# A four-layer transformer on one core: in the first wide attention, the second norm's z and its turn each move one tick later

## The chip, the cores and the metric

The kernel runs on one core of a Trainium2 chip. The metric is the device time of one execution in microseconds (us); the figure of a kernel is the median of its runs. One further execution is recorded by the hardware profiler.

## What is computed

Sixteen sequences of 256 tokens with 128 channels pass through four blocks, each an attention and a feed-forward part on normalised input, added to the stream. The change lies in the first attention alone:

```python
x = x + _L0_attn_ref(_layernorm(x, axis=-1), gamma, w_q, w_kv, null_kv, q_scale, k_scale, w_out)

def _L0_attn_ref(x, gamma, w_q, w_kv, null_kv, q_scale, k_scale, w_out):
    ...
    xn = (x - mu) * jax.lax.rsqrt(var + LN_EPS) * gamma      # the second norm, after _layernorm
    q = (xn @ w_q) ...                                       # 16 heads of 64
    k, v = split(xn @ w_kv)
    ...                                                      # two null keys and values, l2norm of q and k,
    sim = q k^T * 8 + ALiBi, causal                          # softmax
    out = softmax(sim) v
    return out @ w_out
```

So the input is normalised twice, one norm after the other.

## The kernel before, in words

`Core` holds eight stages that run one behind the other; the first is `Wide(self, 0, 0, ...)`, the wide attention of kind 0. It treats the sequences b = 0 to 15 in a software pipeline whose step is called a tick. A sequence has an item "prep" that starts at tick 16b and four items "unit" (four heads each, u = 0 to 3) that start at ticks 16b + 8 + 4u. At each tick every live item issues its part k (ticks since its start). Within a tick the items are sorted by a rank, one for TensorE and ScalarE (`rank`), one for VectorE (`dve_rank`), one for GpSimd (`pool_rank`). The orders are fixed when the program is built; each engine works through its own list in order, and semaphores tie them together.

The prep of sequence b, in the kernel before:

- VectorE k = 0: mean and variance of x (`dve_stats`, L2770 and L2772), two token tiles of 128.
- GpSimd k = 1: 1/sqrt(variance) (`pool_rstd`, L2777 and L2779: an add and a power, per tile).
- VectorE k = 2: the first z (`dve_z`, L2785), then mean and variance of that z.
- GpSimd k = 3: 1/sqrt for the second norm. In tick 3 (mod 4) GpSimd first does a unit's part k = 3 (scale q and k to unit length, L1014 to L1021, and the null scores, L1007 and L1008), then this, then the sum of a unit's output into the stream (L982, four adds).
- VectorE k = 4: the second z (`dve_z`, z <- z), at rank 6, last in its tick.
- TensorE k = 6 (`zT_at`): two 128x128 transposes of z into PSUM (L2764, "ident,z"). ScalarE copies them, times gamma, as the high part of zT (L659); VectorE forms the low part (L797). On VectorE this is rank 1.
- The first user is part "qk" of unit 0 at tick 16b + 8. It waits for the low part (L2756 to L2758, products with wA).

What the engines do in the ticks around it (tick counted mod 16 within the sequence):

- Tick 4, TensorE: pv and row sums, v, qk. VectorE: null maximum, then the second z.
- Tick 5, TensorE: masks, st and mx scores (the last four of each group are "KH,QH"), qk, transposes of S. VectorE: two maxima (L892), squares' sum (L808), L849 and L850.
- Tick 6, TensorE: st and mx scores, **transposes of z**, the out product (L2761, "wO,OT", 16 matmuls), the turn of q (L2764, "ident,raw"). VectorE: two maxima (L892), three small steps on them (L902, L905, L910), **low part of zT**, L808, two products T (L861), low part of q (QL, L816).
- Tick 7, TensorE: turn of nm (L2764, "ident,nm", two transposes), turn of k (four). VectorE: low part of k (KL, L816).
- Tick 8, TensorE: pv ("P,V"), row sums ("P,one"), v, then qk of unit 0 of the new sequence.

PSUM's eight banks are given out in turn (`Psum.take`, ring G), in TensorE's order. A take waits until the reader of the take eight before it is done, since that one had the same bank. In tick 6 of the kernel before, the takes are st, st, mx, mx, zT, Y, Y, turn of q. The eighth take before zT is the first mx of tick 5, which VectorE reads by L892.

For sequence 0 the three VectorE parts of prep stand ahead of the pipeline (`pre_dve`, `is_early`), and `mid_dve` (small constants) stands in tick 7.

Of the kernel before, what the change touches and what calls it, by code (L numbers as in the profile page):

```python
# [29 lines left out]
def fv(a):  # L30
    return a.bitcast(F32)
# [96 lines left out]
class Wide:  # L128
# [9 lines left out]
    def __init__(self, K, s, kind, loads=(), behind=None):  # L138
        self.K, self.s, self.kind = K, s, kind
        self.causal = kind == 0  # L140
        if kind == 0:
            first, last, unit = 8, 13, 24
            self.tk = {"qk": 0, "turn": 6, "mx": 9, "v": 12, "mT": 15, "st": 17, "pv": 20, "sT": 21, "out": 22}
        else:
            first, last, unit = 6, 5, 19
            self.tk = {"turn": 0, "v": 2, "mx": 4, "mT": 7, "st": 8, "pv": 11, "sm": 15, "sT": 16, "out": 17}
        self.apart = (self.tk["st"] - self.tk["mx"]) // 4
        self.zT_at, self.sn_at = (6, 12) if kind == 0 else (4, 99)
        items = []
        for b in range(NSEQ):  # L150
            items.append((16 * b, 0, "prep", (b,), last))
# [118 lines left out]
    def is_early(self, name, a, k):  # L270

        if self.kind == 0:
            return name == "prep" and a[0] == 0 and k in (0, 2, 4)
        return self.kind == 2 and name == "prep" and a[0] < 2 and k in (0, 2, 4)

    def early_pe(self, pe, b, k):
# [486 lines left out]
    def dve_prep(self, dv, b, k):  # L763
        K, s, e = self.K, self.s, dv.e
        n = K.nb[s] + (4 * b if self.kind == 0 else 2 * b)
        za = self.z[(2 * b if self.kind == 0 else b) % len(self.z)]
        zb = self.z[(2 * b + 1) % len(self.z)]
        if self.kind == 2 and b == 0 and k == 3:
            dv.wait_ge(*K.ps.filled("bias"))
            e.tensor_copy(self.bias[:, :], K.ps.ap("bias")[:, 0:128]).then_inc(K.ps.out_of("bias"), 1)  # L770
        if self.kind == 0 and b == 0 and k == 7:
            K.mid_dve(dv)
        if self.kind == 0 and b == 0 and k == 12:
            K.late_dve(dv)
        if k == 0:
            K.x_ready(dv, s, b)
            for i in range(2):
                K.dve_stats(dv, n + i, K.XR[:, 2 * b + i, :])
        if k == 2:
            if self.kind == 2 and b >= 2:  # L780
                dv.wait_ge(*K.ps.filled("zT", s, b - 2))
            for i in range(2):
                K.dve_z(dv, n + i, za[:, i, :], K.XR[:, 2 * b + i, :])
            if self.kind == 0:
                dv.wait_ge(K.zs, n + 2)
                for i in range(2):
                    K.dve_stats(dv, n + 2 + i, za[:, i, :])
        if self.kind == 0 and k == 4:
            if b >= 2:
                dv.wait_ge(*K.ps.filled("zT", s, b - 2))  # L790
            for i in range(2):
                K.dve_z(dv, n + 2 + i, zb[:, i, :], za[:, i, :])
        if k == self.zT_at:
            dv.wait_ge(self.z_hi, b + 1)
            hi, lo, ps = self.zT[b % 3][:, 0:256], self.zT[b % 3][:, 256:512], K.ps.ap("zT", s, b)[:, 0:256]
            if self.kind == 0:
                i = e.scalar_tensor_tensor(lo, ps, K.pc("gamma"), fv(hi), ALU.mult, ALU.subtract)  # L797
            else:
                i = e.tensor_tensor(lo, ps, fv(hi), ALU.subtract)
            i.then_inc(K.ps.out_of("zT", s, b), 1)  # L800

    def dve_unit(self, dv, b, u, k):
        K, s, g, e, kind = self.K, self.s, 4 * b + u, dv.e, self.kind
# [121 lines left out]
    def pool(self, po):  # L925
        K, s, e = self.K, self.s, po.e
        K.stage_free(po, s)
        e.memset(self.one[:, :], 1.0).then_inc(self.one_in, 1)
        if self.kind == 0:
            e.memset(self.nvw[:, :], 0.0).then_inc(self.nv_zero, 1)  # L930
        for name, a, k in self.pool_order:
            if name == "prep":
                n = K.nb[s] + (4 if self.kind == 0 else 2) * a[0]
                if self.kind == 0 and k in (1, 3) and not self.is_early(name, a, k - 1):
                    for i in range(2):
                        K.pool_rstd(po, n + k - 1 + i)
                if self.kind == 2 and k == 0:
                    for i in range(2):
                        K.pool_rstd(po, n + i)
                if k == 3 and self.kind == 2:  # L940
                    self.pool_bias(po, a[0])
            elif name == "behind":
                a[0].pool(po, a[1], k)
            elif name == "ahead":
                K.stages[a[0]].early_pool(po, a[1], k)
            elif name == "null" and k == 2:
                b = a[0]
                xs = K.XR[:, 2 * b:2 * b + 2, :].rearrange("p t c -> p (t c)")
                po.wait_ge(self.summed, 4 * b + 4)
                po.wait_ge(*K.ps.read("nul", s, b))  # L950
                e.tensor_tensor(xs, xs, self.ny[b % 2][:, :], ALU.add).then_inc(self.nulled, 1)
            elif name == "unit":
                if self.kind == 0:
                    self.pool_unit(po, 4 * a[0] + a[1], k)
                elif self.part("st", k - 1) is not None:
                    self.pool_halves(po, 4 * a[0] + a[1], k - 1 - self.tk["st"])
                if k == self.tk["out"] + 1:
                    self.pool_sum(po, *a)
            elif name == "load":
                a[0].pool(po, k)  # L960
# [1632 lines left out]
class Core:  # L2593
# [252 lines left out]
    def pre_dve(self, dv):  # L2846
        e, nk, first = dv.e, self.nk, self.stages[0]
        dv.wait_ge(self.c_in["nk"], 16)
        e.tensor_tensor(nk[:, 16:32], nk[:, 0:16], nk[:, 0:16], ALU.mult).then_inc(self.nk_sq, 1)
        first.dve_prep(dv, 0, 0)  # L2850
        dv.wait_ge(*self.ps.filled("nk2"))
        e.tensor_scalar(nk[:, 160:176], self.ps.ap("nk2")[:, 0:16], 1e-24, None, ALU.max, ALU.bypass).then_inc(
            self.ps.out_of("nk2"), 1)
        self.a0_low(dv, 0).then_inc(self.a0_lo_v, 1)
        first.dve_prep(dv, 0, 2)
        self.a0_low(dv, 1).then_inc(self.a0_lo_v, 1)
        self.a0_low(dv, 2).then_inc(self.a0_lo_v, 1)
        first.dve_prep(dv, 0, 4)
        self.a0_low(dv, 3).then_inc(self.a0_lo_v, 1)
        dv.wait_ge(self.par_in, 16)  # L2860
        e.tensor_scalar(self.qs8[:, :], self.pc("qs"), 8.0, None, ALU.mult, ALU.bypass).then_inc(self.qs8_in, 1)
# [233 lines left out]
```

## Time and profile before

| | before |
|---|---|
| median of 3 runs | 2493.4 us (2490.78 to 2494.09) |
| profiled execution, its own time | 2489.93 us |
| its span, first to last instruction | 2488.3 us |
| TensorE busy, whole span | 93% |
| VectorE / ScalarE / GpSimd busy | 65% / 60% / 64% |
| mean granted TensorE clock | 0.981 of full speed |
| first stage (wide attention) | from the start to about 744 us |
| one sequence in that stage | 46.6 us |

Busy shares are averages over eight different stages. What matters for the change is which engine sets the pace of the first stage and what it waits for there.

### The profile page before, as it was taken

What the parts mean: (1) busy time and instruction counts of PE and PEld (TensorE: products, weight loads), DVE (VectorE), ACT (ScalarE), POOL (GpSimd) and SP (SyncE); (2) the same over time, 40 slices, a digit from 0 to 9 for tenths busy, and PEclk for the clock granted to TensorE, in tenths of its full rate; (3) what the DMA queues carried; (4) which work ended last, traced back from release to release, by engine and by line L of the source; (5) the groups of instructions that cost most, each with busy time, mean ns of one, the idle gap of its engine ahead of it and who ended that gap; (6) DMA issues with size and microseconds to landing.
All of it is one profiled execution on the core that took longest, in us unless ns stands there. A gap on an engine that the chain in (4) does not pass through costs nothing. (4 is left out here: it accounts for less than half of the span.)

```text
span 2488.3 us, 60369 instructions
## 1 busy us (share of the span) xinstructions
PE 2321.6 (93%) x23146; PEld 1789.9 (72%) x23209; DVE 1620.9 (65%) x4106; ACT 1480.6 (60%) x2973; POOL 1588.5 (64%) x2537
## 2 busy tenths in 40 slices
PE   6999999999998999988999999999999968699997
PEld 5778878878876556656777787777778757566665
DVE  5666666666674578874454577777777732478786
ACT  5666666666664478874444466666666523377775
POOL 6788888888885364443333277777777732366664
PEclk9999999999999989999999999999999989899999
DMA  8950000000000010001000000000000036100000
GB/s 284 331 170 2 2 2 2 2 2 2 2 2 1 1 47 2 2 2 33 1 1 1 3 4 4 6 6 4 6 6 4 6 99 182 58 11 10 8 4 35
DMA packets 22911, 83.84 MB, mean 34 GB/s; under 512 B 3969, under 2 KB 10754, under 8 KB 21474
## 3 DMA queue, kind: packets, MB, share of 16 engines
q1 hardware_dynamic: 19474, 72.76, 9.0%
q0 software_dynamic: 3152, 7.21, 0.9%
q8 instruction: 187, 3.06, 0.5%
q14 instruction: 98, 0.80, 0.1%
HBM read 72.75 MB, written 46.79 MB: 48 GB/s over the span
## 5 line engine op out<-in xcount | busy, mean ns | idle before, releaser
L982 POOL TENSOR_TENSOR XR<-XR,T 128x256 f32<-128x256 f32 x504 | 368.4, 731 | 37.7 <-DVE T L861 8.0
L725 ACT ACTIVATE P<-ps 128x384 f32<-128x384 f32 (+1 forms) x512 | 250.5, 542 | 194.8 <-PE ps L2761 191.5
L2761 PE MATMUL ps<-P,V 128*64 128x256 f32 (+3 forms) x4096 | 334.3, 348 | 0.8 <-ACT P L725 0.7
L1529 DVE TENSOR_REDUCE bm<-ps 128x3 f32<-128x384 f32 x512 | 260.3, 550 | 52.4 <-PE ps L2761 49.7
L2761 PEld LDWEIGHTS ps<-P,V 128*64 128x64 f32 (+1 forms) x4096 | 185.9, 123 | 123.1 <-issue 46.3
L1469 ACT ACTIVATE P<-ps 128x768 f32<-128x768 f32 x256 | 207.5, 811 | 76.3 <-PE ps L2761 71.0
L892 DVE TENSOR_REDUCE sm<-ps 128x2 f32<-128x512 f32 (+1 forms) x256 | 129.8, 548 | 168.5 <-PE ps L2761 168.5
L1636 POOL TENSOR_SCALAR_AFFINE_SELECT P<-P 128x512 f32<-128x512 f32 x256 | 165.4, 647 | 103.1 <-ACT P L1469 101.5
L995 POOL TENSOR_TENSOR PS<-P 128x256 f32<-128x256 f32 x256 | 181.3, 732 | 69.1 <-ACT P L725 68.8
L1016 POOL TENSOR_TENSOR ss<-ss,nhalf 128x16 f32<-128x16 f32 x64 | 187.7, 2932 | 5.3
L2761 PE MATMUL ps<-mk,identb 128*128 128x256 bf16 (+1 forms) x768 | 174.8, 296 | 15.2 <-DVE bm L1529 9.0
L2756 PE MATMUL ps<-wA,zT 128*128 128x256 f32 (+1 forms) x544 | 169.0, 311 | 3.2 <-DVE T L861 1.6
L861 DVE TENSOR_TENSOR T<-ps,rs 128x512 f32<-128x512 f32 x252 | 161.2, 681 | 8.3 <-PE ps L2761 7.0
L2761 PE MATMUL ps<-QH,KH 64*128 64x256 f32 (+1 forms) x1024 | 162.1, 313 | 1.0 <-ACT MT L715 0.9
L2779 POOL TENSOR_TENSOR stat<-stat,nhalf 128x1 f32<-128x1 f32 x256 | 149.1, 582 | 21.3
L839 DVE TENSOR_REDUCE nm<-ps 128x2 fp32r<-128x512 f32 x256 | 161.4, 673 | 1.7 <-PE ps L2761 1.7
L1843 POOL TENSOR_TENSOR hr<-hf,hr 128x512 fp32r<-128x512 f32 x48 | 62.1, 1293 | 151.1 <-DVE hr L1832 128.9
L2758 PE MATMUL ps<-wA,zT 128*128 128x256 f32 (+1 forms) x544 | 153.5, 282 | 0.0
L2757 PE MATMUL ps<-wA,zT 128*128 128x256 f32 (+1 forms) x544 | 153.4, 282 | 0.0
L733 ACT ACTIVATE OT<-ps 128x512 f32<-128x512 f32 x128 | 76.5, 597 | 128.8 <-PE ps L2761 128.8
L2761 PE MATMUL ps<-wO,OT 64*128 64x128 f32 x2048 | 149.9, 281 | 2.5 <-DVE sm L892 2.2
L2761 PE MATMUL ps<-QH,KL 64*128 64x256 f32 (+1 forms) x1024 | 144.3, 278 | 0.0
(315 smaller groups left out, 6792.8 us busy)
## 6 DMA issues: line engine op xcount, KB each, us to landing
rows_i<-in_zero SPq DMA_DIRECT2D x16, 1208.0 KB, 30.9
rows_o<-in_zero SPq DMA_DIRECT2D x16, 1208.0 KB, 80.5
w<-in_m_w SPq DMA_DIRECT2D x23, 578.0 KB, 4.0
zt<-rows_i SPq DMA_DIRECT2D x23, 128.0 KB, 3.1
rows_o<-yo POOLq DMA_DIRECT2D x23, 128.0 KB, 3.8
stg<-in_t_w SPq DMA_DIRECT2D x11, 256.0 KB, 2.8
XR<-in_x SPq DMA_DIRECT2D x4, 512.0 KB, 9.2
out<-XR SPq DMA_DIRECT2D x8, 256.0 KB, 2.0
```

What stands on the lines that cost most here:

```text
L725: e.activation(self.P[at % 6][:, :], K.ps.ap("st", s, g, h)[:, 0:self.w], ACT.Exp, bias=0.0, scale=1.0 if kind == 0 else 0.125).then_inc(K ...
L839: e.tensor_reduce(nm[:, :, 64 * par + n], ps[:, :].rearrange("p (t c) -> p t c", t=2), X, ALU.max, negate=True).then_inc(K.ps.out_of("mx", ...
L861: e.tensor_tensor(self.T[g % 2][:, par], K.ps.ap("Y", s, g, par)[:, :].rearrange("p (a t c) -> p a t c", a=2, t=2), r[:, par].unsqueeze(3) ...
L982: p = po.e.tensor_tensor(x, x, self.T[g % 2][:, par, pr], ALU.add)
L995: po.e.tensor_tensor(self.PS[g % 2][:, h, :], P[:, 0:256], P[:, 256:512], ALU.add).then_inc(self.halved, 1)
L1016: d = po.step(e.tensor_tensor(ss[:, 32:48], ss[:, 16:32], K.nhalf[:, 0:16], ALU.pow))
L1469: e.activation(self.P[(2 * g + n) % 6][:, :, 0:384], K.ps.ap("st", s, g, n)[:, :, 0:384], ACT.Exp, bias=0.0, scale=self.scale).then_inc(K. ...
L1529: e.tensor_reduce(bm[:, h, :], K.ps.ap("mx", s, g, h)[:, 0:384].rearrange("p (a c) -> p a c", c=128), X, ALU.max, negate=True).then_inc(K. ...
L1636: e.affine_select(own, own, [[0, 4], [1, 128]], ALU.is_ge, 0.0, base=0, channel_multiplier=-1).then_inc(self.masked, 1)
L2756: self.te.matmul(o, L[0], R[0], start=start, stop=False)
L2758: return self.te.matmul(o, L[0], R[1], start=False, stop=stop)
L2761: return self.te.matmul(o, l, r, start=start, stop=True, skip_group_check=True)
```

## The change

The second z goes from part 4 to part 5 of the prep, and the turn of z with its two copies from part 6 to part 7, in the first wide attention alone (the other wide attention keeps part 4 for its turn). `mid_dve`, which stood in tick 7 of sequence 0, is now called behind the low part of zT in that tick. GpSimd's condition is written another way and takes the same parts.

```diff
-        self.zT_at, self.sn_at = (6, 12) if kind == 0 else (4, 99)
+        self.z2_at, self.zT_at, self.sn_at = (5, 7, 12) if kind == 0 else (99, 4, 99)
...
         if self.kind == 0:
-            return name == "prep" and a[0] == 0 and k in (0, 2, 4)
+            return name == "prep" and a[0] == 0 and k in (0, 2, self.z2_at)
...
-        if self.kind == 0 and b == 0 and k == 7:
-            K.mid_dve(dv)
...
-        if self.kind == 0 and k == 4:
+        if k == self.z2_at:
             if b >= 2:
                 dv.wait_ge(*K.ps.filled("zT", s, b - 2))
             for i in range(2):
...
             i.then_inc(K.ps.out_of("zT", s, b), 1)
+            if self.kind == 0 and b == 0:
+                K.mid_dve(dv)
...
-                if self.kind == 0 and k in (1, 3) and not self.is_early(name, a, k - 1):
+                if self.kind == 0 and k in (1, 3) and a[0] > 0:
...
-        first.dve_prep(dv, 0, 4)
+        first.dve_prep(dv, 0, first.z2_at)
```

Tick 7 then reads: on TensorE turn of nm, transposes of z, turn of k; on VectorE low part of zT, low part of k. Tick 6 has the out product right behind the scores.

## Rows read from the trace of the kernel before

**Rows 1.** The page, part 1: busy time of each engine, share of the span, instructions.
```profile
PE 2321.6 (93%) x23146; PEld 1789.9 (72%) x23209; DVE 1620.9 (65%) x4106; ACT 1480.6 (60%) x2973; POOL 1588.5 (64%) x2537
```

**Rows 2.** Waits from 60 to 740 us: who waited for whom, us, times, longest.
```profile
DVE z L2785 <- POOL stat L2779: 59.0, 32, 4.1
PE ps L2764 <- DVE sm L892: 9.1, 14, 1.2
PE ps L2761 <- DVE sm L892: 2.2, 14, 0.2
```

**Rows 3.** Timeline of TensorE, ticks 5 to 8 of one sequence: start, us, instructions, idle before.
```profile
367.33 0.45 PE L2761 MATMUL ps<-KH,QH 64*128 64x256 f32 x4
...
370.24 0.39 PE L2761 MATMUL ps<-KH,QH 64*128 64x128 f32 x4
371.24 0.44 PE L2764 MATMUL ps<-ident,z 128*128 128x128 f32 x2 [0.62 <-DVE sm L892]
371.84 1.16 PE L2761 MATMUL ps<-wO,OT 64*128 64x128 f32 x16 [0.16 <-DVE sm L892]
...
374.17 1.52 PE L2761 MATMUL ps<-P,V 128*64 128x256 f32 x16
...
377.22 0.28 PE L2756 MATMUL ps<-wA,zT 128*128 128x256 f32 x1
```

**Rows 4.** Timeline of TensorE, the same ticks of a unit without a turn of z.
```profile
335.97 0.39 PE L2761 MATMUL ps<-KH,QH 64*128 64x128 f32 x4
...
337.72 0.38 PE L2764 MATMUL ps<-ident,nm 128*128 128x128 f32 x2
337.94 0.60 PE L2764 MATMUL ps<-ident,raw 128*128 128x128 f32 x4
338.47 1.52 PE L2761 MATMUL ps<-P,V 128*64 128x256 f32 x16
```

**Rows 5.** Timeline of VectorE, ticks 4 to 7 of the sequence of rows 3.
```profile
369.04 0.35 DVE L2785 TENSOR_SCALAR z<-z,stat 128x128 f32<-128x128 f32 x1 [3.49 <-POOL stat L2779]
369.91 0.68 DVE L2785 TENSOR_SCALAR z<-z,stat 128x128 f32<-128x128 f32 x1 [0.53 <-POOL stat L2779]
370.51 1.27 DVE L892 TENSOR_REDUCE sm<-ps 128x2 f32<-128x512 f32 x2
...
372.61 0.70 DVE L892 TENSOR_REDUCE sm<-ps 128x2 f32<-128x256 f32 x2
373.44 0.17 DVE L902 TENSOR_TENSOR sm<-sm,par 128x4 f32<-128x4 f32 x1
...
374.01 0.48 DVE L797 SCALAR_TENSOR_TENSOR zT<-ps,par,zT 128x256 fp32r<-128x256 f32 x1
374.40 0.67 DVE L808 TENSOR_REDUCE ss<-sqr 128x8 f32<-128x512 f32 x1
...
376.85 0.74 DVE L816 SCALAR_TENSOR_TENSOR KL<-ps,par,KH 128x512 fp32r<-128x512 f32 x1
```

**Rows 6.** Timeline of GpSimd beside it: the four adds of a unit's output.
```profile
369.78 3.14 POOL L982 TENSOR_TENSOR XR<-XR,T 128x256 f32<-128x256 f32 x4
```

**Rows 7.** A small VectorE step, all of its line from 60 to 740 us (min/median/max ns).
```profile
L905 DVE TENSOR_TENSOR nm<-sm x58: 167/168/734, 67.5 to 734.0; 128x8 fp32r<-128x8 f32 x58
```

**Rows 8.** Timeline: the longest kind of that step, and GpSimd at that time.
```profile
349.13 0.72 POOL L951 TENSOR_TENSOR XR<-XR,ny 128x256 f32<-128x256 f32 x1 [1.07 <-ACT ny L615]
349.15 0.73 DVE L905 TENSOR_TENSOR nm<-sm 128x8 fp32r<-128x8 f32 x1
```

**Rows 9.** Timeline of TensorE, ticks 6 to 8 of sequence 2.
```profile
88.50 0.39 PE L2761 MATMUL ps<-KH,QH 64*128 64x128 f32 x4
...
94.54 1.52 PE L2761 MATMUL ps<-P,V 128*64 128x256 f32 x16
```

**Rows 10.** Windows, the stretch from 90.6 us: length, busy time and instructions of PE, PEld, DVE, ACT and POOL, then the granted clock.
```profile
90.60:94.00 3.40, 3.33 (x22) 3.11 (x23) 3.16 (x13) 0.59 (x2) 1.40 (x5) 0.50 0.94 330
```

**Rows 11.** Timeline of TensorE, the turn of z of sequence 1.
```profile
46.03 0.50 PE L2764 MATMUL ps<-ident,z 128*128 128x128 f32 x2 [2.44 <-DVE z L2785]
```

## The prediction

> **What bounds the kernel now.** I read the page first, for who is busy. TensorE works 93% of the span, VectorE, ScalarE and GpSimd 60 to 65% [rows 1]. The change touches the first stage only, so I then read the waits of its even part, 60 to 740 us. VectorE stands for 59.0 us, 32 times, at the z of L2785, because GpSimd has not finished 1/sqrt [rows 2]. That is the largest wait that the change addresses, but VectorE isn't the bound, so it is worth nothing by itself. What counts is what reaches TensorE: 14 times it waits for a VectorE maximum ahead of a transpose (9.1 us), and 14 times again ahead of a product (2.2 us) [rows 2]. Fourteen is the number of sequences 2 to 15, so this is one event per sequence.
>
> The timelines show the chain. In tick 4 VectorE reaches the second z and stands 3.49 us, then 0.53 us more, until both 1/sqrt are there [rows 5]. Behind z in its queue are the two maxima of tick 5. Their scores were in PSUM at 367.33 + 0.45 = 367.78 [rows 3], but the maxima start at 370.51 [rows 5]: 2.7 us late. The transposes of z take the PSUM bank of the first of these maxima, so TensorE, ready at about 370.5, turns z only at 371.24, and the out product waits for the second maximum until 371.84 [rows 3].
>
> **What the event costs.** The idle column says 0.62 + 0.16 us, but it starts from a modelled end, so I take starts. From the last scores of tick 6 to "P,V" of tick 8: 374.17 - 370.24 = 3.93 us [rows 3]. A unit without a turn of z needs 338.47 - 335.97 = 2.50 us, and two transposes are 337.94 - 337.72 = 0.22 us [rows 4]. So 3.93 - 2.50 - 0.22 = 1.21 us per sequence are lost. Sequence 2 is worse: 94.54 - 88.50 = 6.04 us [rows 9], 2.11 more; part of it ran at half clock (granted 0.50, the 1.2 GHz level, right behind its stall) [rows 10].
>
> **The change part by part.**
>
> - *Second z, tick 4 to tick 5 on VectorE.* It moves past two maxima, one L808 and two short steps; no instruction is added. The maxima start at about 367.8. The group needs 372.61 - 370.51 = 2.10 us [rows 5], so VectorE comes to z at 369.9, when the second 1/sqrt has just come (the second z began at 369.91, released by it [rows 5]). The 4 us stall goes nearly whole. GpSimd's chain up to there starts from earlier work that doesn't move, so 1/sqrt comes at the same time relative to TensorE.
> - *Transposes, tick 6 to tick 7 on TensorE.* The out product now takes the banks of tick 5's maxima, which are free by about 369.1, and starts at once; the transposes take a bank of tick 6's st scores, read by ScalarE. Their z is done at about 370.9, and they issue near 372.2: 1.3 us of slack. Gain 14 x 1.21 = 16.9 us. Bounds: 14 x 0.78 (the idle column) = 10.9 and 16.9.
> - *Sequence 2's extra 2.11 us.* I take all of it as gone, since the stall ahead of the slow stretch goes. Bounds: 0.6 (only its longer stall) and 2.1.
> - *Sequence 1* waits 2.44 us for z itself [rows 11]. z comes no sooner, but the turn of q (four transposes, 338.47 - 337.94 = 0.5 us [rows 4]) now goes ahead inside that wait. I take 0.5; bounds 0 and 2.4.
> - *The low part of zT and its high copy, tick 6 to tick 7.* On VectorE it moves past L808, two T and QL. This is the cost. TensorE needs it at qk of tick 8: without the stall "P,V" starts at 370.24 + 2.50 + 0.22 = 372.96, and qk 377.22 - 374.17 = 3.05 us later [rows 3], at 376.01. VectorE: the maxima of tick 6 can start at 370.24 + 0.39, about 370.7. From there to KL it took 376.85 - 372.61 = 4.24 us, with the low part (374.40 - 374.01 = 0.39) among it [rows 5]. So it now starts 3.85 us behind the maxima, at 374.55, and ends 0.48 later at 375.0: 1.0 us of slack, if nothing else slows VectorE.
> - *What slows VectorE.* GpSimd's four adds run from 369.78 to 372.92 [rows 6]. In the kernel before, VectorE's two-operand steps L902, L905 and L910 began at 373.44 [rows 5], behind the adds; now they come at 370.7 + 0.83 = 371.5, amid them. L905 takes 168 ns at the median but up to 734 [rows 7], and the long one ends as a GpSimd operation of 0.72 us ends [rows 8]; the z at 369.91 took 0.68 instead of 0.35 beside the first add [rows 5, 6]. If the small steps get through only by 372.92 + 0.4 = 373.3, and L808 would have followed at 370.7 + 1.4 = 372.1, VectorE is 1.2 us late. The low part ends at 376.2. TensorE followed a VectorE end (371.16) by 0.08 us [rows 3, 5], so it waits 0.3 us. Bounds: 0 and 0.7 (half an add more). I take 0.3, because both rows of such an overlap show a full hold. Cost 14 x 0.3 = 4.2 us.
> - *Nothing else.* KL shifts by the low part's 0.39 us and is needed only at tick 9. The high copy shifts one tick on ScalarE, which is idle 40% [rows 1]. GpSimd's list, the DMA queues and SP's queue are unchanged; so is sequence 0's order, since tick 6 and 7 hold nothing else there. `mid_dve` costs nothing for that reason; had it other work beside it, its few copies would delay it by their own length once.
>
> The Trainium skill has a rule here, in "SBUF — State Buffer", section "SBUF: two separate sides": VectorE with two SBUF inputs (or in a two-port mode) and GpSimd take one port pair by an exclusive lock, and the later one waits for the whole instruction. The trace agrees with it where the two overlap [rows 8]. Taken strictly it would hold each z and each small step to the end of an add, which is the rival C below; with no lock at all the sum would be that of rival B.
>
> **Sum.** 16.9 + 2.1 + 0.5 - 4.2 = 15.3 us less. The profiled execution took 2489.9 us (span 2488.3), so it would take 2474.6. It lies 3.5 below the median of the runs shown; the median becomes 2493.4 - 15.3 = 2478.1.
>
> **Rivals.**
>
> - **A, the forecast:** the stall goes and a small wait at qk comes. Chance 0.44.
> - **B, no new wait:** VectorE's small steps slip between the adds (the adds wait for one another, so there are gaps). Gain 19.5, 2473.9 us. For it: 1.0 us of slack without the hold, and most L905 are short [rows 7]. Chance 0.24.
> - **C, the hold is strict:** each z waits for an add, then the small steps for the rest, the adds themselves slipping. The four adds are 0.785 us each; one more of them makes VectorE 2.0 us late, the low part ends at 377.0 and the wait is 1.05 us. Of 1.21 only 0.16 is left: gain 2.2 + 2.6 = 4.8, 2488.6 us. From A on, each 0.1 us that VectorE is later costs 1.4 us over the 14 sequences. Chance 0.16.
> - **D, nothing measurable:** TensorE's gain in this stage is eaten by the next thing late there (masks of tick 9 waiting for KL, now 0.39 us later, or GpSimd). Against it: of 3.93 us lost and spent here, only the waits for the maxima of L892 stand between TensorE's products [rows 3], and no other wait of TensorE in that stretch is as long. 2492 us. Chance 0.09.
> - **E, slower:** one mechanism, the low part of zT comes more than 1.2 us behind TensorE's qk. It decides when it ends after 377.2, 2.2 us later than without any hold; every 0.1 us beyond costs 1.4 us. With 0.5 us beyond, 2493.4 + 7 - 2.6 = 2498 us. Chance 0.07.
>
> **Chances and range.** A measurement of this kernel can tell a change of about 0.2%, 5 us, from none. A and B are faster, C mostly by half, D same, E slower: faster 0.80, same 0.13, slower 0.07. The range goes from B with 2 us for scatter of the runs, 2472, to C's edge at 2488; it leaves out D, E and part of C.
>
> **What the profile would show.** The wait of VectorE z for GpSimd falls from 59 us to under 10. The waits of TensorE for the maxima of L892 (9.1 and 2.2 us) vanish. "KH,QH" to "P,V" falls from 3.93 to 2.7 us. A new row, TensorE's product with wA waiting for VectorE's zT (L797), stands at 14 times 0.3 us (by B it is absent, by C 1 us each). L902 and L905 of tick 6 last 0.3 to 0.7 us. The half-clock stretch at 90.6 us is gone. One sequence takes 46.6 - 0.9 = 45.7 us instead of 46.6. Wrong would be the prediction if z now stands at its new place too (GpSimd late by more than I read), or if zT's low part comes behind other VectorE work that I take as done.

## The result, and the profile after

The changed kernel takes 2479.8 us (median of 4 runs, 2478.6 to 2481.7), the kernel before 2493.7 us beside it: ratio 0.995, 95% interval 0.9938 to 0.9962, 14 us less. A second measurement of the same two kernels (below) gives 2478.9 against 2493.3, ratio 0.9943 (0.9928 to 0.9958). The forecast was 2478.1 us, 15.3 us less. The profiled execution has a span of 2480.0 us; what it shows beyond the first stage is taken up at the end of this section.

The waits of the changed kernel from 60 to 740 us (who waited for whom, us, times, longest), beside [rows 2]:

```profile
PE ps L2761 <- DVE KL L816: 4.4, 15, 1.0
DVE z L2785 <- POOL stat L2779: 2.4, 5, 0.6
PE ps L2756 <- DVE T L861: 1.8, 1, 1.8
PE ps L2756 <- DVE zT L795: 0.4, 1, 0.4
```

VectorE's wait for 1/sqrt fell from 59.0 to 2.4 us, and both waits of TensorE for the maxima (L892) are gone. The page says the same of the span: TensorE 94% instead of 93%.

```profile
PE 2323.5 (94%) x23146; PEld 1793.6 (72%) x23209; DVE 1632.7 (66%) x4106; ACT 1481.6 (60%) x2973; POOL 1592.1 (64%) x2537
```

The timeline of TensorE, the same ticks of a sequence as in [rows 3]:

```profile
362.52 0.39 PE L2761 MATMUL ps<-KH,QH 64*128 64x128 f32 x4
...
364.50 0.38 PE L2764 MATMUL ps<-ident,z 128*128 128x128 f32 x2
...
365.25 1.52 PE L2761 MATMUL ps<-P,V 128*64 128x256 f32 x16
...
367.48 0.38 PE L2756 MATMUL ps<-wA,zT 128*128 128x256 f32 x1
...
368.18 0.28 PE L2758 MATMUL ps<-wA,zT 128*128 128x256 f32 x1
368.58 0.36 PE L2756 MATMUL ps<-wA,zT 128*128 128x256 f32 x1
...
371.09 0.45 PE L2761 MATMUL ps<-KH,QH 64*128 64x256 f32 x4
```

From the last scores to "P,V" it is 2.73 us instead of 3.93: the 1.20 us are all gone. But read on by starts: the products with wA follow each other every 0.12 us, except the one at 368.58, which is the first of qk of the new sequence: 0.40 us behind its neighbour, then one gap of 0.19. "P,V" to the scores of tick 9 takes 371.09 - 365.25 = 5.84 us, and 5.48 in the kernel before. So 0.36 us per sequence come back as a new wait. **No wait is listed at that product**, since its neighbour's modelled end (368.18 + 0.28 = 368.46) leaves only 0.12 us before it; only the starts show it. The period of a sequence is 45.76 us instead of 46.60 (median of the distances of "KH,QH" between 200 and 700 us): 1.20 - 0.36 = 0.84.

VectorE at that time, beside [rows 5], and below it GpSimd, beside [rows 6]:

```profile
362.20 1.48 DVE L2785 TENSOR_SCALAR z<-z,stat 128x128 f32<-128x128 f32 x2
363.60 0.74 DVE L892 TENSOR_REDUCE sm<-ps 128x2 f32<-128x256 f32 x2
364.48 0.16 DVE L902 TENSOR_TENSOR sm<-sm,par 128x4 f32<-128x4 f32 x1
364.67 0.59 DVE L905 TENSOR_TENSOR nm<-sm 128x8 fp32r<-128x8 f32 x1
...
367.31 0.73 DVE L816 SCALAR_TENSOR_TENSOR QL<-ps,qs,QH 128x512 fp32r<-128x512 f32 x1
367.97 0.47 DVE L795 SCALAR_TENSOR_TENSOR zT<-ps,par,zT 128x256 fp32r<-128x256 f32 x1
368.36 0.73 DVE L816 SCALAR_TENSOR_TENSOR KL<-ps,par,KH 128x512 fp32r<-128x512 f32 x1
```

```profile
362.06 3.18 POOL L982 TENSOR_TENSOR XR<-XR,T 128x256 f32<-128x256 f32 x4
```

The low part of zT ends at 368.44, and qk starts at 368.58. The adds run from 362.06 to 365.24. The two z take 1.48 us together, against 0.56 us where the adds are cut (below), and L905, the small step that falls into the last add, takes 0.59 instead of 0.17 and ends with the adds. In narrower windows of the same timeline the single operations show, first z and first add, second z and second add, then the fourth add:

```profile
362.06 0.73 POOL L982 TENSOR_TENSOR XR<-XR,T 128x256 f32<-128x256 f32 x1
362.20 0.67 DVE L2785 TENSOR_SCALAR z<-z,stat 128x128 f32<-128x128 f32 x1
...
362.79 0.89 DVE L2785 TENSOR_SCALAR z<-z,stat 128x128 f32<-128x128 f32 x1
362.87 0.73 POOL L982 TENSOR_TENSOR XR<-XR,T 128x256 f32<-128x256 f32 x1
...
364.48 0.76 POOL L982 TENSOR_TENSOR XR<-XR,T 128x256 f32<-128x256 f32 x1
```

The first z ends at 362.87, the first add at 362.79; the second z ends at 363.68, the second add at 363.60. So each z is held until an add ends and is done 0.08 us later, and L905 ends at 365.26, 0.02 us behind the fourth add. L902 is not held: in the unrounded trace it starts 2 to 8 ns before the fourth add in all 14 sequences. It takes its usual 0.16 us, and that add lasts 0.75 to 0.76 us, against 0.73 for those ahead of it here.

In sequence 1 (timeline of TensorE) the turn of q does go ahead of z, but a wait for the low part follows, so that qk starts at 49.33 (49.70 before):

```profile
46.24 0.41 PE L2764 MATMUL ps<-ident,z 128*128 128x128 f32 x2 [2.29 <-DVE z L2785]
46.49 0.60 PE L2764 MATMUL ps<-ident,raw 128*128 128x128 f32 x4
49.33 0.36 PE L2756 MATMUL ps<-wA,zT 128*128 128x256 f32 x1 [1.53 <-DVE zT L795]
```

The half-clock stretch of sequence 2 is gone; windows (columns as in [rows 10]) of the changed kernel, and below them of one in the second stage and of a new one near the first stage's end:

```profile
80.00:96.00 16.00, 14.96 (x168) 11.83 (x168) 11.77 (x30) 10.00 (x21) 14.66 (x20) 1.00 0.97 323
```

```profile
846.80:884.30 37.50, 34.97 (x218) 22.39 (x220) 23.30 (x54) 21.84 (x41) 21.71 (x30) 0.50 0.24 64
727.30:730.70 3.40, 3.16 (x21) 2.43 (x24) 0.00 (x0) 0.18 (x2) 3.24 (x6) 0.50 0.02 5
```

GpSimd's last add of a sequence into the stream in the first stage (all of L951; first and last start) shows where this execution stands:

```profile
L951 POOL TENSOR_TENSOR XR<-XR,ny x16: 725/726/743, 112.6 to 777.6; 128x256 f32<-128x256 f32 x16
```

It was 116.1 to 790.4 in the kernel before, so the first stage there lasts until about 790 us and not, as the table of the kernel before says, until 744 us. So 3.5 us are gained by the end of sequence 0's unit work (which overlaps sequences 1 and 2), 12.8 us by the end of the stage, but only 8.3 us by the end of the span. With 13 periods of 0.84 us on top of 3.5 the stage would have gained 14.4 us; the missing 1.6 us fit the half-clock stretch at 727.3 us, which the trace of the kernel before doesn't have. In the second stage the longest half-clock stretch lasted 17.1 us in the kernel before and 37.5 us in this one. The other executions don't follow it: the medians differ by 14 us, and a second profile of the same kernel has 13.7 us of half clock there and a span of 2476.5 us. So the lag behind the medians is put down to scatter of one execution, in a stage that the change doesn't touch.

### The profile page after: what moved, and what is told of

It reads as the page before. It is cut to its first block and busy times, and to the rows that moved or that the text cites. A ratio compares the mean times of both kernels' runs of the same rounds, so it can differ in the third digit from the quotient of the medians.

```text
span 2480.0 us, 60369 instructions
## 1 busy us (share of the span) xinstructions
PE 2323.5 (94%) x23146; PEld 1793.6 (72%) x23209; DVE 1632.7 (66%) x4106; ACT 1481.6 (60%) x2973; POOL 1592.1 (64%) x2537
## 5 line engine op out<-in xcount | busy, mean ns | idle before, releaser
L892 DVE TENSOR_REDUCE sm<-ps 128x2 f32<-128x512 f32 (+1 forms) x256 | 130.5, 551 | 203.3 <-PE ps L2761 203.3
L2756 PE MATMUL ps<-wA,zT 128*128 128x256 f32 (+1 forms) x544 | 169.6, 312 | 6.9 <-DVE zT L795 3.0
```

Of the source, the lines that this page charges most:

```text
L2756: self.te.matmul(o, L[0], R[0], start=start, stop=False)
```

## The experiments

Each ran on the same chip as the kernel before, in three sessions in which the kernel before had other medians: 2491.8 us beside the second z alone, the turn alone, the changed kernel with adds cut and the low part first; 2493.3 us beside the changed kernel run again, the low part last, the first z later and both edits together; 2492.7 us beside the kernel before with adds cut. So compare ratios, not times. Three lengths are read from each trace, medians over the ten to twelve sequences between 200 and 700 us: last scores of tick 6 to "P,V" (A), "P,V" to the scores of tick 9 (B), and the period.

| kernel | median, us | ratio (95%) | A | B | period |
|---|---|---|---|---|---|
| before | 2491.8, 2493.3, 2492.7 | 1 | 3.93 | 5.48 | 46.60 |
| changed, run again | 2478.9 | 0.9943 (0.9928 to 0.9958) | 2.72 | 5.81 | 45.72 |
| second z alone | 2490.3 | 0.9997 (0.9985 to 1.0009) | 3.97 | 5.48 | 46.66 |
| turn alone | 2500.7 | 1.0032 (1.0020 to 1.0045) | 4.27 | 5.49 | 46.95 |
| changed, adds cut | 2472.0 | 0.9923 (0.9910 to 0.9936) | 2.72 | 5.49 | 45.40 |
| before, adds cut | 2487.5 | 0.9975 (0.9963 to 0.9987) | 3.59 | 5.49 | 46.28 |
| changed, low part first | 2478.0 | 0.9940 (0.9923 to 0.9957) | 2.72 | 5.66 | 45.58 |
| changed, low part last | 2486.5 | 0.9974 (0.9963 to 0.9985) | 2.72 | 6.47 | 46.38 |
| changed, first z later | 2475.7 | 0.9929 (0.9917 to 0.9941) | 2.72 | 5.89 | 45.43 |
| low part first and first z later | 2472.5 | 0.9919 (0.9907 to 0.9932) | 2.72 | 5.74 | 45.29 |

### One half of the change at a time

The second z alone:

```diff
-        self.z2_at, self.zT_at, self.sn_at = (5, 7, 12) if kind == 0 else (99, 4, 99)
+        self.z2_at, self.zT_at, self.sn_at = (5, 6, 12) if kind == 0 else (99, 4, 99)
```

> The second z goes to tick 5, the turn of z and its copies stay in tick 6. My theory (the change gains because the stalled z held back the maxima of tick 5, whose PSUM banks TensorE needs; it pays with a late low part of zT): the maxima are on time here, but z itself is now done about 0.9 us after TensorE is ready to turn it. From the last scores of tick 6 to P,V it takes 3.6 to 3.8 us (3.93 before, 2.73 changed), the wait changes its name to VectorE z, and the qk of tick 8 doesn't wait. Per sequence 0.1 to 0.3 us less than before, so 2487 to 2492 us. Rival (moving z off the head of VectorE's queue is the whole gain, and the turn's place is indifferent): the time is that of the changed kernel, 2480 us, or 5 us less.

No change: ratio 0.9997. The wait is as long as before and has another name (timeline of TensorE):

```profile
367.61 0.41 PE L2764 MATMUL ps<-ident,z 128*128 128x128 f32 x2 [0.92 <-DVE z L2785]
```

The maxima are no longer late, but TensorE comes to a z that isn't there. A is 3.97 us, 0.2 above my upper figure: the two z last 1.48 us there, beside the adds as in the changed kernel, not the 0.7 I reckoned with. The rival, that this half is the whole gain, is out.

The turn alone:

```diff
+        self.z2_at, self.zT_at, self.sn_at = (4, 7, 12) if kind == 0 else (99, 4, 99)
```

> The second z stays in tick 4, the turn of z and its copies go to tick 7. My theory: the maxima of tick 5 stay 2.7 us late, and now the out product takes both their banks; its first matmul waits for both, until about 371.8 in the time of the rows of before. From the last scores to P,V 4.0 to 4.2 us (3.93 before), no wait at qk since TensorE is as late as VectorE. Time 2493 to 2498 us. Rival (the turn's place makes the gain, since TensorE no longer meets a z that has just come): 2480 to 2485 us.

Slower, ratio 1.0032 (8 us), more than I gave. The out product now stands where the transposes stood and needs the banks of both late maxima:

```profile
377.33 1.16 PE L2761 MATMUL ps<-wO,OT 64*128 64x128 f32 x16 [1.34 <-DVE sm L892]
```

A is 4.27 us, 0.34 longer than before, which over sequences 3 to 15 is 4.4 us; GpSimd's first L951 comes at 119.7 us instead of 116.1, so 3.6 us more are lost in sequences 1 and 2. There this trace has a half-clock stretch of 13.7 us from 46.2 us, and the kernel before one of 3.4 us from the same time; whether the edit brings the longer one isn't shown. So each half alone is worth nothing or less, and both together gain 14 us.

### What makes the low part late

GpSimd's adds of one unit cut to almost nothing, in the changed kernel and in the kernel before; the output of the first attention lacks this unit's share for 14 sequences:

```diff
             for pr in range(2):
-                p = po.e.tensor_tensor(x, x, self.T[g % 2][:, par, pr], ALU.add)
+                if self.kind == 0 and u == 1 and b < 14:
+                    p = po.e.tensor_tensor(x[0:1, 0:1, 0:8], x[0:1, 0:1, 0:8], self.T[g % 2][0:1, par, pr, 0:1, 0:8],
+                                           ALU.add)
+                else:
+                    p = po.e.tensor_tensor(x, x, self.T[g % 2][:, par, pr], ALU.add)
```

> The changed kernel, but GpSimd's four adds of unit 1 into the stream are cut to 8 elements of one partition for sequences 0 to 13 in the first stage, so this part of the output is left out. These adds run beside z and the small steps L902 to L910 of VectorE. My theory (they hold VectorE's two-operand steps, and this is why the low part of zT comes late): the two z take 0.65 us together instead of 1.48, L905 of that tick 0.17 instead of 0.59, and P,V to the scores of tick 9 falls from 5.84 to 5.48 us. Per sequence 0.36 us less, 2474 to 2476 us. Rival (the low part is late only because it stands behind more work of VectorE): P,V to scores stays near 5.8 us and the time at 2480 us. Other products that read the stream are unaffected in their place.

B falls to 5.49 us, the value of the kernel before, and the period to 45.40. VectorE's timeline:

```profile
359.85 0.56 DVE L2789 TENSOR_SCALAR z<-z,stat 128x128 f32<-128x128 f32 x2
...
361.67 0.17 DVE L905 TENSOR_TENSOR nm<-sm 128x8 fp32r<-128x8 f32 x1
...
364.49 0.47 DVE L795 SCALAR_TENSOR_TENSOR zT<-ps,par,zT 128x256 fp32r<-128x256 f32 x1
```

The z and L905 have their short times, and qk doesn't wait, although VectorE's order is the same. The rival, that the low part is late merely because it stands behind more work, is out. The time, 2472.0 us, is 2 us below my lower figure, in a session whose kernel before is some 2 us faster too.

> The kernel before, with the same adds cut to 8 elements (unit 1, sequences 0 to 13, so this part of the output is left out). My theory says that the adds hold the second tile of the second z there too: its 0.68 us become 0.35, the maxima of tick 5 start 0.33 us sooner, and from the last scores to P,V it takes 3.6 instead of 3.93 us. The small steps behind are not held there, so nothing else changes: period 46.3 us, 4 to 5 us less, ratio 0.998. Rival (the adds matter only to the changed kernel, or GpSimd's load slows all in general): the ratio is 1.000, or as large as the 0.36 us per sequence and more that it gave in the changed kernel with P,V to the scores shorter than 5.48 us.

All as expected. The adds held the second tile of z in the kernel before too. All z <- z of either kernel between 85 and 700 us (min/median/max ns): the kernel before, where the first tile of a pair has the short time and the second the long one, and below it with the adds cut.

```profile
L2785 DVE TENSOR_SCALAR z<-z,stat x28: 345/508/677, 87.9 to 696.1; 128x128 f32<-128x128 f32 x28
```

```profile
L2789 DVE TENSOR_SCALAR z<-z,stat x28: 345/346/348, 88.1 to 690.6; 128x128 f32<-128x128 f32 x28
```

In the changed kernel, where both tiles are held, this row reads 311/674/889 ns.

### Where the low part stands

Between T and QL (the transposes stay in tick 7):

```diff
+        self.low_at = 6 if kind == 0 else 4
...
-        return 6 if self.kind == 0 and name == "prep" and k != self.zT_at else self.rank(name, k)
+        if self.kind == 0 and name == "prep":
+            return 2.5 if k == self.low_at else 6
+        return self.rank(name, k)
...
-        if k == self.zT_at:
+        if k == self.low_at:
             dv.wait_ge(self.z_hi, b + 1)
```

> The changed kernel, but VectorE forms the low part of zT at the end of tick 6, between the two T and QL, while the transposes stay in tick 7. My theory: the low part ends 0.66 us sooner, ahead of TensorE's qk, and L905 and z keep their long times. P,V to the scores of tick 9 falls from 5.84 to 5.48 us, 0.36 us per sequence, 2474 to 2476 us. Rival (the 0.36 us are not a wait for the low part, but for KL or a PSUM bank): 5.84 us stay, 2480 us. Second rival (VectorE now waits for ScalarE's high part at that place and QL and KL slip): new waits for L816, 2480 us or more.

Half of what I expected: B is 5.66 us, not 5.48, and by its interval the time (2478.0 us, not 2474 to 2476) isn't distinct from the changed kernel's. qk no longer waits; VectorE's KL ends where it did, and the next thing that needs it stops instead. VectorE's KL, and below it TensorE's first product of qk and the masks of tick 9:

```profile
368.98 0.74 DVE L819 SCALAR_TENSOR_TENSOR KL<-ps,par,KH 128x512 fp32r<-128x512 f32 x1
```

```profile
368.96 0.28 PE L2759 MATMUL ps<-wA,zT 128*128 128x256 f32 x1
...
369.87 0.38 PE L2764 MATMUL ps<-mk,identb 128*128 128x256 bf16 x2
```

KL ends at 369.72, the masks start at 369.87, 0.15 us later, much as qk started 0.14 us behind the low part. So moving the low part alone gives back 5.84 - 5.66 = 0.18 of the 0.36 us, and the other 0.18 are met by a second wait, which the first had covered.

Behind KL, the last of tick 7:

```diff
+        return 6 if self.kind == 0 and name == "prep" else self.rank(name, k)
```

> The changed kernel with VectorE's low part of zT at the end of tick 7, behind KL, 0.66 us later. It doubles the cost that the forecast named. My theory (TensorE's qk waits for exactly this copy): P,V to the scores of tick 9 goes from 5.85 to 6.5 us, the period to 46.4 us, and with 14 x 0.66 = 9 us more the time is 2487 to 2490 us, ratio about 0.999. Rival (the 0.36 us are a wait for the bank of KL alone): KL is 0.39 us earlier here, and P,V to the scores falls to 5.5 us, ratio 0.993.

B is 6.47 us, 0.66 more than in the changed kernel run beside it, the distance from one step of this kind to the next (367.31 to 367.97 above); the period is 46.38. The time is at the lower edge of what I gave, and the ratio 0.9974 instead of about 0.999. The rival with KL's bank is out as the sole cause. The wait is now long enough to be listed:

```profile
PE ps L2756 <- DVE zT L795: 10.7, 14, 1.0
```

> The changed kernel once more, on the same chip and against the same runs of before as the three others. All theories: period 45.76 us, ratio 0.994 to 0.996.

### A further wait of the same kind

The first z with its statistics goes from part 2 to part 3, behind KL of that tick:

```diff
+        self.z1_at = 3 if kind == 0 else 2
...
-            return name == "prep" and a[0] == 0 and k in (0, 2, self.z2_at)
+            return name == "prep" and a[0] == 0 and k in (0, self.z1_at, self.z2_at)
...
-        if k == 2:
+        if k == self.z1_at:
...
-        first.dve_prep(dv, 0, 2)
+        first.dve_prep(dv, 0, first.z1_at)
```

> The changed kernel, and the first z with the statistics of it goes from part 2 to part 3 on VectorE, so that in tick 2 it no longer stands between the low part of q (QL) and the low part of k (KL). My theory: the 4.4 us that TensorE waits for KL in tick 5, 15 times (0.37 us each by starts), go; GpSimd's 1/sqrt of the second norm is not later, since it stands behind a unit's work there. Period 45.4 us instead of 45.76, 5 us less than the changed kernel, ratio to before about 0.993. Rival (the wait for KL is only the first of two, masks of tick 5 also wait for something else): the period stays at 45.7 us.

> Both: the low part of zT ahead of QL as in the run with that edit alone (period 45.58 us), and the first z a part later. My theory: the two are independent waits and add, period 45.2 us, ratio to before about 0.992. Rival (they share slack): 45.4 us or more, not below the first z alone.

The first gives the 0.3 us: period 45.43 against 45.72 of the changed kernel run beside it, ratio 0.9929. TensorE's waits for KL in the even part fall from 15 to one, while the wait for the low part of zT is now long enough to be listed 12 times (B is 5.89 us):

```profile
PE ps L2757 <- DVE zT L796: 2.5, 12, 0.8
PE ps L2757 <- DVE T L862: 1.8, 2, 1.6
PE ps L2762 <- DVE KL L817: 1.0, 1, 1.0
```

Both edits together have a period of 45.29 us and a ratio of 0.9919, the fastest full kernel here and clear of the kernel before. By the periods the two edits add: 45.72 - 0.29 - 0.14 = 45.29 (I had expected 45.2). The intervals of the times overlap, of this kernel with that of the first z alone and of both with that of the changed kernel run beside them, so what each edit gives is shown by the period only.

## Why the prediction was right

- **The chain.** Late 1/sqrt, stalled z, late maxima, a bank that TensorE needs: each link was in the rows, and the two halves of the change confirm it. With the z off VectorE's head the wait becomes one for z; with the turn moved but z left, the out product inherits the banks.
- **The stall's size by starts, 1.21 us.** Measured 3.93 - 2.73 = 1.20. The idle column (0.62 + 0.16) would have given 10.9 us for 14 sequences where 16.8 went.
- **The new wait, 0.3 us.** Measured 0.36, so 5.0 us over 14 sequences instead of 4.2. The low part ended 368.44 - 362.52 = 5.92 us behind the last scores, forecast 376.2 - 370.24 = 5.96. The reason given, steps of VectorE held by GpSimd's adds, is shown by the kernels with the adds cut. But the 1.2 us of lateness were made up of other parts than I wrote. I put all of them on the small steps L902 to L910. In fact the z lost most: the pair takes 1.48 against 0.56 us, and the maxima of tick 6 start 363.60 - 362.52 = 1.08 us behind the scores, where I had 0.46 (370.7, which also lies ahead of the 370.9 at which my own z ends). L905 lost 0.42, L902 nothing. Two errors of about 0.6 us each cancelled, so that the wait came out so near is in part luck. TensorE also followed the low part by 0.14 us and not by 0.08.
- **Sequence 2, 2.1 us.** From the last scores to "P,V" it now takes 2.72 us instead of 6.04, so the 2.1 us are gone in this pair of traces, less 0.26 us because the wait for the low part is 0.62 us there. Some 0.6 of the 2.1 is a longer stall: "turn alone" and "before, adds cut" have it too (4.83 against 4.27, 4.18 against 3.60). The other 1.5 is the half-clock stretch, and these two kernels have the stall there without it. So that the change removes it is not shown; one trace of each kernel can't tell.
- **Sequence 1, 0.5 us.** From its last scores to those of sequence 2 it takes 45.03 us instead of 45.35, so 0.3 less, but not for the reason given. TensorE reaches v at 46.84 instead of 48.32, because the turn of q went ahead and because a half-clock stretch of the kernel before (46.2 to 49.6 us, granted clock 0.50), which I had overlooked, isn't there. Then it waits for the low part of zT and has lost nearly all of it when qk starts (49.33 against 49.70). I had no wait for the low part in this term. In the second profile of the changed kernel the same distance is 44.44 us, so a term of 0.5 us lies within the scatter of single executions.
- **Sum.** By starts, 16.8 + 2.1 + 0.3 - 5.3 = 13.9 us (5.3 with sequence 2's longer wait); forecast 15.3, measured 14.0 and 14.4. In the traces the changed kernel is another 0.4 us ahead before its first turn of z; with it the gain at sequence 3 is 137.22 - 133.74 = 3.5 us, as GpSimd's first L951 shows. Moving `mid_dve`, which I took to cost nothing, has no run of its own.
- **Rivals.** B (no new wait) is what the kernel with the adds cut does: 0.9923 is 19 us, its figure 19.5. C (a strict hold) had the mechanism: each z is held to the end of an add and L905 to the end of the last, and only L902 slips in. But its price was wrong, 1.05 us per sequence instead of 0.36: it made VectorE 2.0 us late, measured 1.2. So the size of the wait is that of A, and the strict hold is that of C. D did not occur, but its masks that wait for KL exist, 0.18 us behind the first wait. E did not occur; the slope given for it, 1.4 us per 0.1 us of lateness, is that of the low part put last: 0.66 us cost 7.6 us by the medians, 9.2 by the slope.
- **What I said the profile would show** was wrong in two places. I named a new row "L2756 waits for zT" at 14 times 0.3 us, though I had just said that idle time counts from a modelled end. The row lists one wait of 0.4 us, that of sequence 2. And L902 kept its 0.16 us, because it started just ahead of an add.

## What to carry to other kernels

Measure a stall of a pipelined engine by the starts of the same instructions with and without it, not by the idle column, which here hid 0.4 of 1.2 us and then a whole wait of 0.36 us. Where buffers go round in a fixed order, a late reader on one engine stops whoever takes its buffer next, so moving the late work and moving that taker are one change: each alone gained nothing. And before a step is moved into a gap of one engine, look at what the other engines do at that time: here the z found GpSimd's adds there and took 1.48 us instead of 0.56.

## What the runs showed of the hardware

Some VectorE operations between SBUF tiles wait for a GpSimd tensor operation that runs beside them: the 128x128 z (a TENSOR_SCALAR) takes 0.68 instead of 0.35 us, and L905 (two SBUF inputs, 128x8) 0.59 beside an add and up to 0.73 [rows 8] instead of 0.17. Others don't: the reduction L808, with one SBUF input, takes as long beside an add as without one. The kernel before, in a narrow window of the timeline:

```profile
371.39 0.73 POOL L982 TENSOR_TENSOR XR<-XR,T 128x256 f32<-128x256 f32 x1
371.71 0.67 DVE L808 TENSOR_REDUCE ss<-sqr 128x8 f32<-128x512 f32 x1
```

Away from the adds it takes 0.67 too [rows 5]. The Trainium skill ("SBUF — State Buffer", section "SBUF: two separate sides") states an exclusive lock on a shared port pair; the trace agrees with it. What I had not expected is how little of a held operation is left once the add has ended: all 27 held z of the changed kernel between 85 and 745 us end 0.08 us behind an add, though a z takes 0.35 us, and the held L905 end 0.02 to 0.03 us behind a GpSimd operation. So a hold costs less than waiting out the add and then running: two z beside four adds in a row take 1.48 us instead of 0.56, 0.9 us more and not two adds more (1.57).
